# Cosine products and sums placed chunk by chunk between the rounds of the X3-row loop

## What is computed

```python
x = _layernorm(x + _L0_gnn_ref(x, ...))
x = _layernorm(x + _L1_gnn_ref(x, ...))
x = _layernorm(x + _L2_gnn_ref(x, L2_gnn_beta, src, dst))
x = _layernorm(x + _L3_gnn_ref(x, ...))

# _L2_gnn_ref
xn = x * jax.lax.rsqrt(jnp.sum(x * x, axis=-1, keepdims=True) + eps)
att = beta[0] * jnp.sum(xn[row_index] * xn[col_index], axis=-1)
m = jax.ops.segment_max(att, row_index, num_segments=N)
e = jnp.exp(att - m[row_index])
denom = jax.ops.segment_sum(e, row_index, num_segments=N)
alpha = e / jnp.maximum(denom[row_index], 1e-16)
out = jax.ops.segment_sum(alpha[:, None] * x[col_index], row_index, num_segments=N)
```

## Time and profile before

| | us |
|---|---|
| median of three runs | 3591.15 |
| the three runs | 3590.56, 3591.15, 3596.0 |
| the profiled execution, its own time | 3587.35 |
| its span in the trace | 3585.5 |
| DVE busy | 2253.2 (63% of the span) |
| POOL busy | 2333.2 (65%) |
| PE busy | 1175.5 (33%) |

### The profile page before, as it was taken

The page is one execution under the profiler, slowest core; times in us unless marked ns, Lnnn a source line. Parts: engine busy times, 40 slices in busy tenths (PEclk is TensorE's granted clock), DMA queues, the critical chain, the costliest instruction groups (busy, mean ns, idle before and its releaser), DMA issues. The chain is left out here.

```text
span 3585.5 us, 33479 instructions
## 1 busy us (share of the span) xinstructions
PE 1175.5 (33%) x5638; PEld 870.0 (24%) x5638; DVE 2253.2 (63%) x4830; ACT 1172.6 (33%) x3423; POOL 2333.2 (65%) x2220
## 2 busy tenths in 40 slices
PE   0555555472122055633552000000000008882221
PEld 0444444362122044521221000000000006661221
DVE  4877777577577477836995333336884436557553
ACT  0666666421223145513552222221000006551110
POOL 6777777777772577327752777774027767772777
PEclk9877877755555555556876555555555559785555
DMA  2677777642111144424662555552001117771000
GB/s 49 204 220 216 222 220 217 202 131 59 42 45 40 41 123 134 122 67 121 201 187 81 151 154 152 153 148 79 0 19 34 48 49 223 218 224 45 18 18 17
DMA packets 247009, 420.84 MB, mean 117 GB/s; under 512 B 75747, under 2 KB 83251, under 8 KB 245677
## 3 DMA queue, kind: packets, MB, share of 16 engines
q1 hardware_dynamic: 176014, 354.96, 32.3%
q0 software_dynamic: 70912, 65.07, 9.2%
HBM read 185.19 MB, written 236.81 MB: 118 GB/s over the span
## 5 line engine op out<-in xcount | busy, mean ns | idle before, releaser
L230 POOL DMA_INDIRECT edge_rows<-x_rows,norm_s x400 | 431.6, 1079 | 141.1 <-issue 121.3
L804 PE MATMUL banks<-ident,cross_in 125*65 125x125 f32 (+4 forms) x26 | 11.2, 431 | 1145.5 <-DVE cross_in L827 751.6
L246 POOL DMA_INDIRECT out_dram<-n_out,scat_i x200 | 224.1, 1120 | 129.0 <-DVE n_out L2145 67.0
L246 POOL DMA_INDIRECT x_rows<-r_x,src_scat_i x200 | 222.6, 1113 | 125.5 <-DVE r_x L2050 63.4
L804 PEld LDWEIGHTS banks<-ident,cross_in 125*65 125x65 f32 (+4 forms) x26 | 3.9, 150 | 1151.1 <-DVE cross_in L827 753.9
L634 DVE TENSOR_REDUCE n_var<-n_sq 125x8 f32<-125x512 f32 x125 | 85.7, 686 | 306.9 <-ACT n_sq L648 306.8
L230 POOL DMA_INDIRECT edge_rows<-in_x_dram,dst_i x200 | 221.0, 1105 | 60.9 <-issue 60.9
L907 DVE TENSOR_TENSOR_SCAN x_t<-x_t 125x144 f32<-125x144 f32 x500 | 202.1, 446 | 82.5 <-ACT x_t L898 74.7
L230 POOL DMA_INDIRECT tops<-norm_rows,src_i x200 | 208.4, 1042 | 68.9 <-issue 67.4
L246 POOL DMA_INDIRECT norm_rows<-edge_rows,scat_i x200 | 208.7, 1043 | 67.9 <-issue 64.5
L230 POOL DMA_INDIRECT edge_rows<-x_rows,key_i x200 | 198.8, 994 | 77.4 <-issue 60.6
(11 more groups left out here) (451 smaller groups left out, 4685.5 us busy)
## 6 DMA issues: line engine op xcount, KB each, us to landing
h_rows<-r_h SPq DMA_DIRECT2D x125, 462.0 KB
x_rows<-r_x SPq DMA_DIRECT2D x125, 241.5 KB
x_rows<-r_x SPq DMA_DIRECT2D x125, 224.0 KB
r_x<-x_rows SPq DMA_DIRECT2D x125, 224.0 KB
x_rows<-n_out SPq DMA_DIRECT2D x125, 224.0 KB
n_in<-in_x_dram SPq DMA_DIRECT2D x100, 224.0 KB
x_mixed_edge_rows<-e_dup SPq DMA_DIRECT2D x50, 448.0 KB
r_x<-x_rows SPq DMA_DIRECT2D x50, 241.5 KB
```

What stands on the lines that cost most here:

```text
L230: g.indirect_dma_start(out=to[:, j, :], out_offset=None, in_=table, in_offset=bass.IndirectOffsetOnAxis(ap=idx[:, j:j + 1], axis=0)).then_ ...
L246: g.indirect_dma_start(out=table, out_offset=bass.IndirectOffsetOnAxis(ap=idx[:, j:j + 1], axis=0), in_=frm[:, j, :] if len(frm.shape) == ...
L804: pe.transpose(crossings["bank"][0:cols, 0:rows], frm, ident[0:rows, 0:rows]).then_inc(s_tout, 1)
```

## The change

`x3_dve` takes a range of rounds, and `dots_dve` takes one chunk. The block now alternates. `X3_CUTS` tells how many rounds have been done before each group's wait: 11, 24, 37, 50, 58 and, for the last group, all 63. Behind the wait, each chunk of dots is followed by one round, as long as rounds are left. So the 25 chunks stand in the list like this: chunks 0 to 3 from round 11 on, 4 to 8 from 24, 9 to 13 from 37, 14 to 18 from 50, 19 to 22 from 58, and chunks 23 and 24 behind the last round. Stretches of rounds without dots are still loops; the mixed parts are written out. The temporary tiles of the products are `n_c[0]`, `n_c[1]` and `n_in[0]`, since `n_sq` is in use by the rounds. Nothing is computed that was not computed before, and nothing is left out. No other engine's list changes.

```diff
-        def x3_dve(dve):
+        def x3_dve(dve, start, end):
...
-            pairs(nc.vector, X3CH, body, v)
+
+            if end - start == 1:
+                body(start, range(min(U, X3CH - 2 * start)))
+                return
+            if start == 0:
+                body(0, range(2))
+            first, links = max(start, 1), v.n
+            with nc.vector.Fori(first, end) as i:
+                v.base, v.n = (i - first) * U + links, 0
+                body(i, range(2))
+            v.base, v.n = 0, links + (end - first) * U
...
-        def dots_dve(dve, products, chunks):
-
-            start = v.n
-            with nc.vector.Fori(chunks[0], chunks[1]) as i:
-                v.base, v.n = (i - chunks[0]) * 2 + start, 0
-                for tmp, a, b, _ in products:
-                    other = tall(b) if len(b.shape) == 2 else b[:, bass.ds(i * NC, NC), :]
-                    done = dve.tensor_tensor(tmp[:, :, :], a[:, bass.ds(i * NC, NC), :], other, ALU.mult)
-                v.link(done)
-                for tmp, _, _, to in products:
-                    done = dve.tensor_reduce(to[:, bass.ds(i * NC, NC)], tmp[:, :, :], AX, ALU.add)
-                v.link(done)
-            v.base, v.n = 0, start + 2 * (chunks[1] - chunks[0])
+        def dots_dve(dve, products, i):
+
+            cols = slice(i * NC, i * NC + NC)
+            for tmp, a, b, _ in products:
+                done = dve.tensor_tensor(tmp[:, :, :], a[:, cols, :], b[:, cols, :], ALU.mult)
+            v.link(done)
+            for tmp, _, _, to in products:
+                done = dve.tensor_reduce(to[:, cols], tmp[:, :, :], AX, ALU.add)
+            v.link(done)
...
+        X3_CUTS = (11, 24, 37, 50, 58)
...
-                x3_dve(dve)
+                products = ((n_c[0], xr, xr, tops[0]), (n_c[1], xc, xc, tops[1]), (n_in[0], xr, xc, heads[0]))
+                at, x3_rounds = 0, (X3CH + 1) // 2
                 for n, (start, end) in enumerate(groups):
+                    to = X3_CUTS[n] if n < len(X3_CUTS) else x3_rounds
+                    if at < to:
+                        x3_dve(dve, at, to)
+                        at = to
                     dve.wait_ge(s_got[n], got_done(n, 5))
-                    dots_dve(dve, ((n_sq[0], xr, xr, tops[0]), (n_sq[1], xc, xc, tops[1]), (n_in[0], xr, xc, heads[0])),
-                             (start, end))
+                    for i in range(start, end):
+                        dots_dve(dve, products, i)
+                        if at < x3_rounds:
+                            x3_dve(dve, at, at + 1)
+                            at += 1
```

## The result

The changed kernel takes 3499.67 us (median of four runs, 3494.64 to 3501.83) against 3593.57 us for the kernel before on the same chip. The ratio of the two kernels is 0.9724, with an interval of 0.9699 to 0.9749 (the two medians alone divide to 0.9739). The forecast was 3512, with a range of 3499 to 3530: the change is faster, and the median lies 12 us under the forecast, at the very bottom of the range. The profiled execution is 3494.64 us with a span of 3492.6 (before: 3587.35 and 3585.5).

The account below looks back on a forecast made before the run. The dots set the end while DVE had idled before them; POOL's gathers were the next limit. Dots ending at 2492.0 instead of 2571.1, with 9.7 us charged to POOL, gain 79.1 us: 3591.15 - 79.1 = 3512, range 3499 to 3530.

Parts of the forecast that it names:

- Rounds that cost nothing: X3 rounds on DVE: a 3.95 us chunk fits the idle gaps, so rounds are charged nothing and stay 8.1 us.
- The cover named: Gaps before `n_var`: buffer 1's late load hides the chunk's overrun of 0.7 to 0.95 us, leaving 0.75 us of second gap.
- Rival 2: X3 rounds grow with the dots; at 2.0 us a chunk the gain is 54, the median 3537; chance 0.05.
- POOL's term: POOL's gathers beside the dots' products: 0.42 us lost per chunk, 9.7 us for 23 chunks; range nothing to 23 us.
- Rival 1: POOL's gathers lose nothing to the dots: gain 88.8 us, median 3502; chance 0.17.
- The waits at groups: DVE's waits for gather landings: none at groups 0 to 3, 15.4 us at group 4; last `n_out` ends at 2477.4.
- What ends last: Stage end: POOL's last landing at 2484.1, 6.7 us after the rounds, then two chunks of 7.9 us; dots end 2492.0.
- The rest moves along: Roots, scans and softmax behind the dots keep their durations and all move forward by the 79.1 us gained.
- Rival 3: POOL held through whole runs of three products, 2 us a chunk: gain 43, median 3548; chance 0.08 including mixtures.

Follow-up runs that it names:

- f3: Changed kernel with the dots of chunks 0 to 22 computed twice, the second time right behind the first: 3536.75 us in one run.
- e3: Changed kernel with each group's chunks of dots together in one gap instead of one per following round: 3551.7 us, ratio 0.9913.
- g3: Changed kernel with an unused sum of 248 numbers ahead of each chunk's products, first product 0.93 us behind the second `n_out`: 3510.08 us, ratio 0.9777.
- f2: Changed kernel with the dots' products replaced by one-input sums and their sums by maxima, cosines left out: 3501.8 us, ratio 0.9758.
- e1: The changed kernel again, without an edit, timed beside the kernel before: 3499.88 us, ratio 0.9754.
- f1: Changed kernel with chunk 23 gathered in group 4, the last group of one chunk, fifth cut at 60: 3503.8 us, ratio 0.9760.
- h1: Changed kernel with seven gather groups, chunks 23 and 24 each in a group of its own, fifth cut at 60: 3498.13 us, ratio 0.9737.
- h2: As h1, with seven groups, but the fifth cut at 59 rounds instead of 60: 3493.41 us, ratio 0.9723.
- g1: Changed kernel with an unused sum of 288 numbers ahead of each chunk's products, first product 0.97 us behind the second `n_out`: ratio 0.9749.

## Where the prediction failed, and what it had right

**Rounds that cost nothing: right.** The period is 8.14 us against 8.13. A chunk is 3.85 us where 3.95 was taken. The cover named was the late load of buffer 1 and the second gap; f3 showed its size (one chunk and 1.5 us), and e3 showed that it is not enough for several chunks. Rival 2 (2 us a round) has nothing for it.

**POOL's term: the step that failed.** The sum charged 3 x 0.14 = 0.42 us a chunk, 9.7 us for 23 chunks. Measured are 1.97 and 1.20 us in the two profiles, and the gathers ended 521.0 and 519.6 us behind t0, where the forecast put them at 528.8. The mechanism was right: a product does hold a gather (0.18 us at 2156.32, up to 0.50 in g3), and f2, without products, has no such waits. The size was a mean from `n_out` multiplies, moved to products as if each instruction met the gathers at a random moment and paid for itself. Neither holds. A held gather is released 0.57 us behind the start of the product, and the next one comes when the third product lets it pass, so a chunk holds one gather at most. At a random moment of the 1.255 us from one gather to the next that would be some 0.28 us a chunk, 6.4 us for 23 (an estimate from these distances). And the moment is not random: the `n_out` pair just ahead has set when the next gather starts, and in this kernel that start falls late in the first product (0.19 us) or on the handover to the third (nothing). So 0.42 us a chunk was too much for an even spread and more so for this placement, which pays 0.05 to 0.09; with the products 0.32 us later, in g3, it is 0.37. The lower end of the term, nothing, was the nearer one.

**Rival 1 (POOL loses nothing) came nearest in time and was wrong in cause.** It had a gain of 88.8 us; the stage gained 87.5 and 88.8. Its cause, that products hold no gather, is refuted by the gathers of 1.13 and 1.45 us shown above. The rule behind it is that of the Trainium skill, "SBUF — State Buffer", section "Who interferes with whom": a `tensor_tensor` with two SBUF inputs was not seen to hold up the writing of descriptors. These traces disagree with it, in that the writing of indirect gathers is held here. Whether a gather reads SBUF, in which case the section's own rule would have the two contend, no run here shows. What the same section says of `tensor_reduce`, that on this chip it never contends, the trace agrees with: in f2 the waits beside the dots are 0.

**The waits at groups: right in place, half the size.** Nothing is waited for at groups 0 to 3. At group 4 it was 7.8 us (6.7 in e1) instead of 15.4, and of the 7.6 us between them 6.8 are the earlier landing of group 4 (480.5 behind t0 instead of 487.3), of which the failed POOL term makes up 6.0 (8.0 charged for 19 chunks, 2.0 paid), and 0.8 are DVE's later arrival. The last `n_out` came at 516.4 instead of 523.7.

**What ends last: right.** The last landing is 1.5 us behind the last gather (1.6 taken), DVE has waited 6.1 us for it (6.7 said), and two chunks of 7.65 us follow (7.9). The steps add up to 521.0 + 1.5 + 7.7 = 530.2, against 528.8 + 1.6 + 7.9 = 538.3: 7.8 us of the difference are POOL's, and 0.3 are the shorter tail.

**The rest moves along: right.** 1014.2 us before, 1010.9 and 1013.7 after. Together: 8 us of the 12 by which the time fell short of 3512 are the POOL term, and the remaining 4 are within what the starts and the later stages scatter, as e1 showed. The same goes for the ratio: 0.9724 stands for some 99 us, more than the stage gained (87.5), and e1 with 0.9754 and 88 us agrees with the stage.

**The other readings.** Rival 3 took the gather of 2.45 us as one beside a product alone; as f2 showed, its wait goes on 0.40 us into the instruction behind the product. The sum does not use it. With 9.7 replaced by 1.2 to 2.0 the sum gives a gain of 87 us and 3504.

## What to carry to other kernels

Work moved into an engine's idle gaps was free here up to the size of the gap and of the slack in the next one, and it was worth spreading it one piece to a gap: here the spreading was 49 us of 88. When the stall of one kind of instruction is carried over as a mean price to another place, ask what fixes the phase there; where an instruction just ahead synchronises both engines, the same instructions can cost 1.2 us in one placement and 8.6 in another. When the last landing sets the end, shrink what stands behind it, but move the cuts with it, or the wait or the leftover pieces take its place (f1, h1, h2).

## What the runs showed of the hardware

- A gather that starts in a DVE `TENSOR_TENSOR` of 512 numbers (`n_out` or a product) is held until 0.55 to 0.57 us behind that instruction's start, not for its whole 0.69 us, and takes 0.95 us from there (2154.50 and 2156.02). A sum of the same size (`TENSOR_REDUCE`, f2) does not hold it. That is not a matter of one input: a `COPY` with one input held an indirect scatter for 0.24 us.
- A held gather fixes the start of the next one: 1.82 us behind the start of the instruction that held it. So the waits are not independent, and no chunk of three products held more than one gather.
- At the handover between two products, 0.605 us apart, a gather gets in for nothing; DVE pays 0.04 to 0.05 us for it (0.73 instead of 0.68, 1.33 instead of 1.28). A few hundredths of a microsecond decide: 0.01 us into the product the gather took 0.95 us, 0.05 us into it 1.45. Behind the wait at group 4, where DVE had been idle, one that started 0.04 us into the product still took 0.96 us, and two products 1.36.
- So a shift of DVE's products by 0.04 us (g1 to g3) changes the gathers' waits from 2.8 to 8.6 us in the pass, and they come back within 0.8 us when the same kernel is run again (1.97 and 1.20, 4.65 and 4.52). Over all kernels with the products at 0.61 they lie between 1.0 and 3.3 us.
- The waits at `n_out` scatter from 13.3 to 17.7 us between runs of kernels whose rounds are the same. Why is open: nothing here sets where the gathers stand when the first round begins.
